# A two-layer AdaLN transformer on one core: the second layer's attention with a centred output projection and its normalisation on ScalarE, other loads and orders, and an unread product in the first attention

## Time and profile before

| what | value |
|---|---|
| median of 3 runs | 556.45 us (550.97 to 559.31) |
| the profiled execution | 555.68 us, span 554.0 us |
| PE busy | 432.3 us, 78% of the span |
| VectorE busy | 372.9 us, 67% |
| ScalarE busy | 270.0 us, 49% |
| GpSimd busy | 253.3 us, 46% |
| TensorE clock granted, mean | 0.896 |

### The profile page before, as it was taken

The page is one execution under the profiler, slowest core; times in us unless marked ns, Lnnn a source line. Parts: engine busy times, 40 slices in busy tenths (PEclk is TensorE's granted clock), DMA queues, the critical chain, the costliest instruction groups (busy, mean ns, idle before and its releaser), DMA issues.

```text
span 554.0 us, 11056 instructions
## 1 busy us (share of the span) xinstructions
PE 432.3 (78%) x2525; PEld 319.0 (58%) x2525; DVE 372.9 (67%) x1197; ACT 270.0 (49%) x710; POOL 253.3 (46%) x322
## 2 busy tenths in 40 slices
PE   4887853097999993788988888897965969899950
PEld 3665741097999993345645645655543547667740
DVE  6876664043656664488999999999867524556546
ACT  3254530053555551557767768767450225555540
POOL 4105357022544444334637576566477003556560
PEclk9998755587999998789999999999987889999995
DMA  8802123856566793852130700000015220222107
GB/s 239 226 17 58 41 58 75 151 145 166 160 183 192 211 322 76 212 126 57 38 96 19 160 29 21 2 20 21 11 34 77 48 46 25 75 73 73 53 13 227
DMA packets 58513, 53.67 MB, mean 97 GB/s; under 512 B 9677, under 2 KB 47358, under 8 KB 58323
## 3 DMA queue, kind: packets, MB, share of 16 engines
q1 hardware_dynamic: 52418, 42.97, 30.9%
q0 software_dynamic: 5056, 8.48, 4.6%
q10 hardware_dynamic: 976, 1.52, 1.5%
HBM read 41.15 MB, written 13.73 MB: 99 GB/s over the span
## 4 chain that ended last, share of the span: by engine, by line
PE 39%; DVE 29%; issue 14%; SPq 6%; DMA 5%; ACT 3%; another core or an unknown queue 2%; POOL 1%; DVEq 0%; POOLq 0%; ACTq 0%
PE bank L1690 7%; PE bank L1683 5%; PE bank L1698 5%; PE bank L1865 4%; DVE qk_sums L1315 3%; PE bank L1730 3%; PE bank L1831 3%; DVE work L1308 2%; PE bank L1789 2%; DVE big L1308 2%; DVE work L1352 2%; PE bank L1857 2%; PE bank L1675 2%; SPq L545 2%
## 5 line engine op out<-in xcount | busy, mean ns | idle before, releaser
L784 POOL DMA_INDIRECT results<-work x94 | 92.0, 978 | 138.9 <-issue 54.8
L1730 PE MATMUL bank<-late,work 128*128 128x512 f32 x192 | 94.3, 620 | 2.4 <-ACT work L950 2.2
L928 ACT ACTIVATE work<-bank,mcol 128x128 f32<-128x128 f32 x94 | 43.0, 457 | 84.7 <-PE bank L1675 75.6
L1683 PE MATMUL bank<-work,big 128*128 128x128 f32 x376 | 52.9, 287 | 0.0
L1262 DVE TENSOR_SCALAR work<-bank,b_columns 128x128 f32<-128x128 f32 x94 | 28.7, 346 | 35.5 <-PE bank L1683 29.0
L1730 PEld LDWEIGHTS bank<-late,work 128*128 128x128 f32 x192 | 33.9, 196 | 31.4 <-issue 28.1
L1698 PE MATMUL bank<-big,work 128*128 x376 | 50.8, 279 | 0.1
L1269 DVE TENSOR_TENSOR work<-bank,bias_big 128x352 f32<-128x352 f32 x47 | 24.7, 525 | 37.5 <-PE bank L1690 35.0
L1683 PEld LDWEIGHTS bank<-work,big 128*128 128x128 f32 x376 | 48.8, 203 | 0.3 <-ACT work L928 0.3
L775 POOL DMA_INDIRECT sorted_tokens<-late,router_at x32 | 31.2, 975 | 38.4 <-DVE late L1211 17.6
L1698 PEld LDWEIGHTS bank<-big,work 128*128 128x128 f32 x376 | 46.9, 196 | 0.3 <-issue 0.3
(11 more groups left out here) (237 smaller groups left out, 1026.9 us busy)
## 6 DMA issues: line engine op xcount, KB each, us to landing
big<-in_W SPq DMA_DIRECT2D x47, 256.0 KB
work<-sorted_tokens SPq DMA_DIRECT2D x94, 65.0 KB
big<-in_w SPq DMA_DIRECT2D x48, 88.0 KB
big<-results SPq DMA_DIRECT2D x16, 256.0 KB, 2.8
sorted_tokens<-zeros SPq DMA_DIRECT2D x26, 65.0 KB
late<-in_WqkvbT SPq DMA_DIRECT2D x1, 1544.0 KB
results<-work POOLq DMA_INDIRECT x94
bias_big<-in_b1e SPq DMA_DIRECT2D x16, 88.0 KB
```

The costliest lines, as they stand in the source:

```text
L784: pool.indirect_dma_start(ys[l], bass.IndirectOffsetOnAxis(xg[b][:, D:D + 1].bitcast(I32), 0), yo[b], None, bounds_check=TOPK * T - 1, oob ...
L928: act.activation(xgT[b % 2], bank[:, ends[b % 2], 0:P], ACT.Identity, bias=scale_shift[0], scale=scale_shift[1]).then_inc(e_xTc, 1)
L1683: last = pe.matmul(hidden_half(b, c), w1r[t % NW][:, c * P:(c + 1) * P], xgT[b % 2], start=True, stop=True)
L1730: last = pe.matmul(bank[:, 2 * k + i, :], h3T[b], Wqkvb[:, k * HD + i * 512:k * HD + (i + 1) * 512], start=True, stop=True)
```

## The change

- `LEAD` goes from 4 to 2.
- The zeros lie in 128 partitions, one row each; a DMA of zeros is now 128 pieces of 520 bytes.
- w2 and b2 of layer 1 are loaded in 4 pieces each (4 experts a piece) at SyncE's steps 1 to 4, ahead of and between the other loads, on a semaphore of their own; the loop of SyncE is written out. Their product with the gate vector is GpSimd's: 8 pieces of 88x512 and 8 of 128x256 in steps 6 to 13 of the second attention. The one GpSimd operation of 88x4096 and VectorE's of 128x2048 behind it go.
- W_o has the mean of its output columns subtracted once, and the residual enters the output product through `cent`, the identity less 1/128, in place of the identity. The row in PSUM has then mean zero, and ln4 needs the sum of squares alone: ScalarE's `Square` with an accumulated sum, Ln, Exp, and a `Copy` with the scale, one behind another. VectorE loses `measure4`, `moments4`, `scale4`; three operations that make `cent` and the centred W_o are new, once.
- The router's modulated rows are written to `hT` at once; `keep` goes. The rows of ones for the shared expert's bias come from ScalarE (they were two memsets of VectorE).
- The lists of VectorE, ScalarE, GpSimd and PE in the second attention have new orders and lags, and the lists of the last tiles after them too. PE's list is the old cycle begun at another stage.
- In the first attention PE has ahead of every query a product of 256 columns of `hT` with WQ, into bank 0, which the query then overwrites.

```diff
-        NW, LEAD = 8, 4
+        NW, LEAD = 8, 2
-        ZR = 8
-        zeros = sb("zeros", [P // ZR, ZR * RW])
+        zeros = sb("zeros", [P, RW])
...
+        def ln_squares(act, n, src, t, b):
+            act.wait_ge(d_o, t + 1)
+            after(act, d_y, 3 * (t - 2) + 1)
+            act.activation(n["xn"][b], src, ACT.Square, accum_out=n["mv"][:, b, 0:1]).then_inc(n["moments"], 1)
+        def ln_root(act, n, t, b):
+            act.wait_ge(n["moments"], t + 1)
+            act.activation(n["r"][:, b, 0:1], n["mv"][:, b, 0:1], ACT.Ln, bias=eps[:, :],
+                           scale=1.0 / D).then_inc(n["rstd"], 1)
+            act.wait_ge(n["rstd"], 2 * t + 1)
+            act.activation(n["r"][:, b, 1:2], n["r"][:, b, 0:1], ACT.Exp, scale=-0.5).then_inc(n["rstd"], 1)
+        def ln_rescale(act, n, src, t, b):
+            act.wait_ge(n["rstd"], 2 * t + 2)
+            act.activation(n["xn"][b], src, ACT.Copy, scale=n["r"][:, b, 1:2]).then_inc(n["normed"], 1)
...
@@ -334,15 +351,20 @@
             after(pe, r["h"], t)
             pe.transpose(r["xT_ps"], r["ln"]["xn"][t % len(r["ln"]["xn"])], ident[:, :]).then_inc(r["xT"], 1)
+        def turned(r, t, b):
+            return hT[:, t * P:(t + 1) * P] if r["layer"] else r["hb"][:, b % 2, :]
         def act_modulate(act, r, t, b):
             act.wait_ge(r["xT"], t + 1)
-            after(act, r["logits"], t - 1)
-            act.activation(r["hb"][:, b % 2, :], r["xT_ps"], ACT.Identity,
+            if r["layer"] == 0:
+                after(act, r["logits"], t - 1)
+            act.activation(turned(r, t, b), r["xT_ps"], ACT.Identity,
                            bias=r["ss"][0], scale=r["ss"][1]).then_inc(r["h"], 1)
         def pe_logits(pe, r, t, b):
             pe.wait_ge(r["h"], t + 1)
...
                 n = table(engine, counts, 0, T)(a, 8)
                 for i in range(8):
-                    eng.dma_start(xs[l][bass.ds(n[i] + (a + i) * REGION, P), :].rearrange("(p k) w -> p (k w)", k=ZR),
-                                  zeros[:, :]).then_inc(z_sent, 16)
+                    eng.dma_start(xs[l][bass.ds(n[i] + (a + i) * REGION, P), :], zeros[:, :]).then_inc(z_sent, 16)
...
@@ -667,10 +689,17 @@
                         sp.dma_start(w13v[:, e, k, :], w[e, :, :].rearrange("e d h -> d e h")).then_inc(ld_w1, 16)
                         sp.dma_start(bv[:, e, k, :], bias[e, :].rearrange("(a e) h -> a e h", a=1)
                                      .to_broadcast([P, 1, H1])).then_inc(ld_w1, 16)
-                    sp.dma_start(w2s.rearrange("p (e c d) -> p e c d", e=E, c=2)[:, e, :, :],
-                                 w2[e, :, :].rearrange("e (c p) d -> p e c d", p=K1)).then_inc(ld_w1, 16)
-                    sp.dma_start(b2B[:, :].rearrange("p (e d) -> p e d", e=E)[:, e, :],
-                                 b2e[e, :].rearrange("(a e) d -> a e d", a=1).to_broadcast([P, 1, D])).then_inc(ld_w1, 16)
+                def outputs1(t, b, q):
+                    if t >= OUTPUT_LOADS:
+                        return
+                    n = E // OUTPUT_LOADS
+                    sp.dma_start(w2s.rearrange("p (e c d) -> p e c d", e=E, c=2)[:, n * t:n * (t + 1), :, :],
+                                 w2[n * t:n * (t + 1), :, :].rearrange("e (c p) d -> p e c d", p=K1)).then_inc(ld_silu, 16)
+                    sp.dma_start(b2B[:, :].rearrange("p (e d) -> p e d", e=E)[:, n * t:n * (t + 1), :],
+                                 b2e[n * t:n * (t + 1), :].rearrange("(a e) d -> a e d", a=1)
+                                 .to_broadcast([P, n, D])).then_inc(ld_silu, 16)
                 def results(t, b, q):
@@ -689,7 +718,7 @@
                 if l == 0:
                     sp.wait_ge(e_o, SLOTS)
                     sp.wait_ge(e_yo, SLOTS)
-                    run_tiles(sp, NT, 4, [(0, results), (2, weights1)])
+                    run_unrolled(NT, 4, [(0, results), (1, outputs1), (2, weights1)])
                 else:
...
+            def scale_outputs(t, b, q):
+                if t >= PIECES:
+                    return
+                if t == 0:
+                    pool.wait_ge(ld_silu, 16 + 32 * OUTPUT_LOADS)
+                n = E // PIECES
+                w = w2s.rearrange("p (e d) -> p e d", d=D)[:, 2 * n * t:2 * n * (t + 1), :]
+                pool.tensor_tensor(w, w, gB[0:K1, 1, 1, :].unsqueeze(1).to_broadcast([K1, 2 * n, D]),
+                                   ALU.mult).then_inc(w2_scaled, 1)
+                w = b2B[:, :].rearrange("p (e d) -> p e d", d=D)[:, n * t:n * (t + 1), :]
+                pool.tensor_tensor(w, w, gB[:, 1, 1, :].unsqueeze(1).to_broadcast([P, n, D]),
+                                   ALU.mult).then_inc(w2_scaled, 1)
             run_unrolled(NT, 4, [
-                (10, double1), (8, residual), (6, product), (11, send1(1)), (11, send1(0)), (1, add_results)], NT + 6)
...
-            pool.wait_ge(ld_w1, 96 * E)
-            w = w2s.rearrange("p (e d) -> p e d", d=D)
-            pool.tensor_tensor(w, w, gB[0:K1, 1, 1, :].unsqueeze(1).to_broadcast([K1, 2 * E, D]),
-                               ALU.mult).then_inc(w2_scaled, 1)
+                (5, residual), (0, add_results), (10, send1(0)), (6, double1), (3, product), (8, send1(1)),
+                (6, scale_outputs)])
...
-            def keep(t, b, q):
-                act.wait_ge(router1["h"], t + 1)
-                act.copy(hT[:, bass.ds(t * P, P)], router1["hb"][:, b % 2, :]).then_inc(f_in, 1)
...
+            def squares4(t, b, q):
+                ln_squares(act, ln4, attn1, t, b)
+            def root4(t, b, q):
+                ln_root(act, ln4, t, b)
+            def scale4(t, b, q):
+                ln_rescale(act, ln4, attn1, t, b)
             run_unrolled(NT, 4, [
-                (3, negatives(1, d_k, 2)), (2, hidden1), (3, exponentials(1)), (7, keep),
-                (4, values_turned), (6, deviation5), (1, deviation3), (2, negatives(0, d_q, 0)),
-                (2, exponentials(0)), (2, beta_parts), (6, modulate1), (4, deviation4)], NT + 3)
+                (4, beta_parts), (6, squares4), (6, root4), (6, scale4), (4, exponentials(0)), (8, modulate1),
+                (7, deviation5), (4, negatives(1, d_k, 2)), (3, hidden1), (4, exponentials(1)),
+                (5, values_turned), (2, deviation3), (3, negatives(0, d_q, 0))], NT + 4)
...
+            link(dve.tensor_scalar(cent[:, :], ident[:, :], -1.0 / D, None, ALU.add))
+            link(dve.reduce_sum(wo_sums[:, :], Wo[:, :, :], AX_X))
+            link(dve.scalar_tensor_tensor(Wo[:, :, :], wo_sums[:, :].unsqueeze(2).to_broadcast([P, HD // P, D]), -1.0 / D,
+                                          Wo[:, :, :], ALU.mult, ALU.add))
             for c, (a, m) in enumerate(SC):
...
-            def measure4(t, b, q):
-                dve.wait_ge(d_o, t + 1)
-                ln_stats(dve, ln4, attn1, t, b)
...
-            def scale4(t, b, q):
-                after(dve, d_y, 3 * (t - 2) + 1)
-                ln_scale(dve, ln4, attn1, t, b)
...
-            def moments4(t, b, q):
-                ln_moments(dve, ln4, t, b)
...
             run_unrolled(NT, 4, [
-                (3, feature(1)), (3, feature_sums), (7, picks[2]), (3, sums_product),
-                (6, norm5), (3, sigmoid_product), (3, sigmoid_inverse), (0, measure3), (3, sigmoid), (4, measure4),
-                (7, picks[3]), (3, qk_reduced), (4, moments4), (7, picks[4]), (3, coefficient), (1, scale3),
-                (3, weighted), (7, places[0]), (2, feature(0)), (4, scale4), (5, measure5), (5, moments5),
-                (0, moments3), (6, picks[0]), (7, places[1]), (7, places[2]), (6, picks[1])], NT + 3)
+                (3, sigmoid_inverse), (3, sigmoid), (3, qk_reduced), (5, moments5), (3, coefficient), (1, scale3),
+                (3, weighted), (7, places[0]), (2, feature(0)), (5, norm5), (0, measure3), (6, picks[0]),
+                (7, places[1]), (4, measure5), (0, moments3), (6, picks[1]), (7, places[2]), (2, feature(1)),
+                (2, feature_sums), (6, picks[2]), (2, sums_product), (6, picks[3]), (2, sigmoid_product),
+                (6, picks[4])], NT + 3)
...
             slots_as_row(1)
-            dve.wait_ge(ld_w1, 96 * E)
-            link(dve.tensor_tensor(b2B[:, :].rearrange("p (e d) -> p e d", e=E), b2B[:, :].rearrange("p (e d) -> p e d", e=E),
-                                   gB[:, 1, 1, :].unsqueeze(1).to_broadcast([P, E, D]), ALU.mult))
             shared_add(1)
...
+            dve.wait_ge(ld_w1, 64 * E)
+            dve.wait_ge(w2_scaled, 2 * PIECES)
...
+            def spare_product(t, b, q):
+                after(pe, b_qT, t)
+                pe.matmul(bank[:, 0, 0:2 * P], Wa[:, 0, :], hT[:, BAND:BAND + 2 * P], start=True, stop=True)
             run_unrolled(NT, 4, [
-                (0, outside_products(0)), (0, outside_products(1)), (6, router_logits0), (0, query),
```

(15 more changed lines are left out.)

69 lines of the change are left out of this document (29 added, 40 removed).

## The result

The changed kernel takes 547.65 us (median of four runs, 544.53 to 551.66), the kernel before 555.46 beside it (four runs, 550.97 to 559.31): a ratio of 0.9891 with a 95% interval of 0.9843 to 0.9938. It is 1.1% shorter where I forecast 2.9%: clear of the spread of the runs, but less than the 2% that the prediction took as the least that can be told from no change. The profiled execution took 546.3 us (span 544.6), before 555.7 (554.0).

A forecast was written before the change was run, and what follows sets the result against it. VectorE was taken to bound the second attention (47.60 of 50 us busy). Shared expert -10, zero rows -5, unread product +4, second attention -4, tail memsets -1 summed to -16: 555.7 to 539.7 us, own range 530 to 547.

The forecast's parts named there:

- The pieces: Second attention, eight w2 and b2 scaling pieces on GpSimd: +4 us, from nothing to 14 if VectorE must wait for each.
- The first rival: Second attention: VectorE pays GpSimd's scaling pieces in full, +14 in place of +4, total 550 us; chance 0.18.
- ln4's three operations: Second attention: VectorE loses three operations per tile, of which 0.6 us a tile counts, -8 us.
- ScalarE did not become the bound: Rival, second attention: ScalarE's four dependent operations become the bound, +21 in place of -4, total 565 us; chance 0.06.
- The shared expert: Layer 1's shared expert: without GpSimd's large product, VectorE's stall goes and PE keeps its clock, -10 us (ends 8 and 10.5).
- the low clock behind the pause: Shared expert: PE came out of the pause at the low clock; without it eight records take 2.5 us less than 5.91.
- The zero rows: Between first attention and its experts: 128 partitions and `LEAD` 2 speed zeros to 288 GB/s, -5 us (ends 0 and 8).
- not within one: Expected sign in layer 0: the first expert load comes within a microsecond of the slot table.
- the part that I had given back: First experts: slot 0's gain of about 1.5 us from `LEAD` 2 is lost as PE waits for slot 8's weights.
- The unread product: First attention: an extra 256-column PE product per tile costs 8.8 us if all shows; half taken, +4 (lower end -3).
- the held clock: Rival, first attention: the extra product holds PE's clock, worth -3 in place of +4, total 533 us; chance 0.07.

## Why the forecast of 540 was 8 us low

**The pieces: the step that failed.** I took +4, "nearer to nothing, since most of VectorE's time is spent on operations that read PSUM or reduce". The runs show 12.5 in eight tiles, almost the upper end of 14. The share of time was the wrong measure: the pieces don't fall anywhere in the tile but behind GpSimd's product, which is bound to VectorE's head sums, or behind a scatter, and there stand exactly the operations that wait. Over all 15 tiles it is 11.4, as a tile ahead of the pieces happened to be 1.1 us shorter in this profile; in the profile without the unread product the pieces cost the eight tiles 14.1. The first rival, pieces paid in full, was the case; its 550 is near the profiled 546.3, and I had given it 0.18. By the Trainium skill ("SBUF — State Buffer", Who interferes with whom) a VectorE operation with two operands in SBUF waits for the whole of a GpSimd operation that reads SBUF. The trace agrees for pieces with two operands (1.17 us in place of 0.17), and for features and head sums that don't wait; it differs for pieces with one operand, beside which such products took 0.17 to 0.52 us.

**ln4's three operations: right in size, not all theirs.** A tile without pieces is 9.73 us, 0.6 below 10.33, as forecast, and 15 tiles gain 8.3 us (146.07 against 154.40). Putting operations of their kinds back costs 0.36 a tile; the rest of the 0.6 lies in the reordered lists or in what the substitutes can't copy, and wasn't parted. ScalarE did not become the bound.

**The shared expert: right.** -9.6 against -10, and the one product put back behind the loop brings the 8.2 us and the 31.6 us stage back. I had the low clock behind the pause right too: the granted clock is 1.00 from 418 to 434 us, where it was 0.50 from 426 to 432 before, and PE's chain now has eight records in 3.63 us in place of 5.91:

```profile
420.86 3.63 PE bank L1819 x8
...
427.89 5.15 PE bank L1819 x12
```

**The zero rows: they move faster, and little of it arrives.** Windows of the changed kernel that answer to the earlier trace rows:

```profile
98.00:100.00 2.00, 1.01 (x4) 0.34 (x4) 0.50 (x3) 0.00 (x0) 0.30 (x1) 0.50 0.75 165
100.00:102.00 2.00, 0.37 (x1) 0.18 (x1) 0.64 (x2) 0.00 (x0) 0.00 (x0) 0.50 0.60 134
```

165 GB/s at a share of 0.75 is 220 at a full one, against 108 before; I had 288 from the stores. But the first expert load came at 103.32, 2.5 us behind the table (100.87) and not within one: SyncE still issues zero rows until 102.5, and then the rows wait for the last of them to land, as the chain and the timeline show.

```profile
102.48 3.20 DMA sorted_tokens<-zeros
...
126.26 2.81 DMA big<-in_W
129.11 0.48 PE bank L1705
```
```profile
103.32 1.22 SPq L660 DMA_DIRECT2D big<-in_W  x2
...
106.15 2.44 SPq L653 DMA_DIRECT2D work<-sorted_tokens  x3
...
108.23 0.45 PE L1705 MATMUL bank<-ident,work 128*128 128x128 f32 x1 [6.93 <-DMA work<-sorted_tokens]
```

PE starts slot 0 at 108.23 instead of 110.66 and slot 8 at 129.11 instead of 129.21: it waits for slot 8's weights again, the part that I had given back, and that gave back nearly all of the 2.4 us by then. The -4.4 of the table is counted from a cast that came 2.6 later; against the clock on the wall the results' load came 1.8 us earlier.

**The unread product: +4 forecast, nothing that shows.** The cast was 2.6 us later in this profile, but 91.6 to 95.2 in others with the product and 92.0 to 93.7 without it. I had priced its time and put the held clock aside as a rival; the clock is shown, and within the spread of the runs the two cancel. By the Trainium skill ("TensorE: Matmul & The Clock Gate", Part 1) activity releases the clock; the trace agrees for the first copy, and shows no more of it for the second. What spoke against the rival, PE full at 0.50 from 58 to 62, is a clock that had already fallen and says nothing on whether more work ahead of it would have kept it up. Nor was the clock 1.2 GHz all the way from 50 us on, as I read it: in the kernel before it is 0.80 from 62 to 66 and 1.00 from 66 to 70.

The sum by the measured terms: -9.6 shared expert, -8.3 lists and ln4, +11.4 pieces over the 15 tiles, -4.4 and +2.6 ahead of them, -1.1 in the rest, -9.4 in all. That the zero rows at -5 and the product at +4 hardly moved the forecast is luck: neither term shows in the totals, and the two errors cancel.

## What to carry to other kernels

Where two engines can hold each other, don't average over an engine's time: see which operation stands beside the added one in each tile, since engines tied by semaphores meet at the same few places every time. Moving an added operation can also push back the next one of its engine, and that one may hold the other engine in its turn (3.2 us here). Work that must be done once belongs on an engine, and into a stage, where it waits: here VectorE did all the pieces between the shared expert's gates for nothing, and the kernel fell to 0.958 to 0.964 of the time before. Zero rows that left from more partitions moved faster here, but a gain at the first slot counts only as far as the next refill of weights is not the later one.

## What the runs showed that I had not expected

A GpSimd operation with two operands in SBUF lengthened VectorE's 16-column product from 0.17 to 1.17 us; with one operand, by another instruction and itself longer (1.53 us on the mean in place of 1.27), it let the same kind of product through in 0.17 to 0.52 us. An unread product of 256 columns raised the granted clock of the first attention (50 to 80 us) from between 0.61 and 0.71 to between 0.75 and 0.88, and a second one did not raise it further (0.81) but cost some 4 us.
